# Sending rows with long ties to a late batch, and one looped copy of the repeat round, in a top-p attention kernel

## The reference, cut to what matters

```python
def _top_p_attention(X, W1, W2, W3):
    logits = (X @ W1.T @ W2.T) @ (X @ W3.T).T
    probs = softmax(logits, axis=-1)
    idx = argsort(-probs, axis=-1)
    sp = take_along_axis(probs, idx, axis=-1)
    cs = cumsum(sp, axis=-1)
    keep_sorted = cs - sp < 0.9          # the fewest largest that reach 0.9
    A = probs * mask(keep_sorted)
    return A / A.sum(-1)
for n in range(2):
    A = _top_p_attention(Xa, W1, W2, W3)
    Xf = R @ Xf                          # R: adj + I, rows normalized
    Xa = A @ Xa
    Z = Z + Xf @ U1[n].T + Xa @ U2[n].T
```

## Time and profile before

| | us |
|---|---|
| median of 3 runs | 2774.62 (2766.83 to 2774.76) |
| the profiled execution | 2770.99 |
| its span | 2769.2 |
| PE busy | 2355.1 (85%) |
| DVE busy | 2199.7 (79%) |
| ACT busy | 1072.5 (39%) |
| POOL busy | 141.5 (5%) |
| mean granted TensorE clock | 0.934 of full |

### The profile page before, as it was taken

One profiled execution on the slowest core, in us unless ns is written; L12 is line 12 of the kernel. 1 busy time (PEld: TensorE's weight loads), 2 busy tenths in 40 slices (PEclk: granted clock), 3 DMA queues, 4 the chain that ended last, 5 costly groups with the idle time before them and its releaser, 6 DMA issues. The chain is left out here.

```text
span 2769.2 us, 53551 instructions
## 1 busy us (share of the span) xinstructions
PE 2355.1 (85%) x17759; PEld 1987.9 (72%) x17759; DVE 2199.7 (79%) x6636; ACT 1072.5 (39%) x1785; POOL 141.5 (5%) x353
## 2 busy tenths in 40 slices
PE   5899998777888887888886649996999999999985
PEld 1566666555767776777775549995999999999952
DVE  2777777279888888888889777766999999999836
ACT  4566666433333333333333130003343443434423
POOL 0000000101111110000000010000000000000000
PEclk9999999997999998999997869998999999999997
DMA  3000000020222221222220235543334343433220
GB/s 128 2 2 1 1 1 2 1 89 17 95 100 100 100 100 51 100 100 101 100 100 14 87 128 202 202 164 127 126 108 143 101 146 104 141 110 134 94 88 25
DMA packets 57106, 245.00 MB, mean 88 GB/s; under 512 B 6705, under 2 KB 18352, under 8 KB 43120
## 3 DMA queue, kind: packets, MB, share of 16 engines
q1 hardware_dynamic: 56816, 241.94, 24.9%
HBM read 235.10 MB, written 6.82 MB: 87 GB/s over the span
## 5 line engine op out<-in xcount | busy, mean ns | idle before, releaser
L1932 PE MATMUL a_acc<-H,pT 128*128 128x128 f32 x4056 | 547.8, 277 | 11.7 <-ACT a_rows L1964 3.8
L1932 PEld LDWEIGHTS a_acc<-H,pT 128*128 128x128 f32 x4056 | 495.3, 192 | 28.7 <-DVE pT L2066 19.9
L935 PE MATMUL small<-XR,wT 128*128 128x128 f32 x2756 | 375.9, 282 | 28.3 <-ACT wT L1131 27.5
L71 DVE MAX8 cand<-e 128x8 f32<-128x64 f32 (+3 forms) x1898 | 302.7, 240 | 101.4 <-issue 101.2
L819 PE MATMUL lg<-kT,qs 128*128 128x512 f32 (+1 forms) x742 | 339.9, 596 | 50.5 <-ACT e L1075 38.5
L935 PEld LDWEIGHTS small<-XR,wT 128*128 128x128 f32 x2756 | 341.6, 196 | 44.4 <-ACT wT L1131 44.4
L2066 DVE TENSOR_TENSOR pT<-a_tr,a_adjT 128x512 f32<-128x512 f32 (+1 forms) x546 | 316.3, 643 | 22.5 <-PE a_tr L1891 19.3
L839 PE MATMUL accR<-XR,adj 128*128 128x129 f32 x2704 | 327.2, 283 | 0.0
L839 PEld LDWEIGHTS accR<-XR,adj 128*128 128x128 f32 x2704 | 324.1, 200 | 0.0
L1891 PE MATMUL a_tr<-ident,prob 128*128 128x128 f32 x2028 | 311.2, 274 | 10.9 <-ACTq L1958 10.9
L1131 ACT ACTIVATE wT<-tr 128x512 f32<-128x512 f32 (+1 forms) x371 | 206.2, 566 | 273.1 <-PE tr L925 271.4
(11 more groups left out here) (334 smaller groups left out, 2457.1 us busy)
## 6 DMA issues: line engine op xcount, KB each, us to landing
adj<-in_adjT SPq DMA_DIRECT2D x52, 1664.0 KB, 7.3
g_adj<-in_adjT SPq DMA_DIRECT2D x26, 1664.0 KB, 6.9
a_adj<-in_adj SPq DMA_DIRECT2D x26, 1664.0 KB, 6.8
a_adjT<-in_adjT SPq DMA_DIRECT2D x156, 256.0 KB, 3.9
a_adjT<-in_adjT SPq DMA_DIRECT2D x26, 128.0 KB, 4.2
XT<-in_x_t SPq DMA_DIRECT2D x1, 1664.0 KB, 13.5
hT_scratch<-hT SPq DMA_DIRECT2D x1, 1664.0 KB, 12.2
nsT_scratch<-nsT SPq DMA_DIRECT2D x1, 1664.0 KB, 5.8
```

What stands on the lines that cost most here:

```text
L71: eng.max(cand[:, n, :], src[:, n * seg:min((n + 1) * seg, width)])
L935: mm = eng.matmul(accA[:, :], wT[(k * NC + c - 1) % 2][:, o:o + P], xa[:, j, 0:P], start=(j == 0), stop=(j == T - 1))
L1932: mm = eng.matmul(acc[:, :], pT[g % RING][:, (j % 4) * P:(j % 4 + 1) * P], H[:, j, :], start=(j == 0), stop=(j == T - 1))
```

## The change

1. `end` computes `late`, whether a partition's own `counts[:, 1, 0:1]` is over 80 (`ROOM_FOR_TIES`). Where `late` is 0, the `backward` rows that are known are counted as open too (`gone`), so that they ask for a slot in the batch, and `backward` becomes 0 for `strict` and `cut_dropped`. The levels are taken with `sharp`, the old `strict`. The three sums of `counts` stand after this.
2. `assign_slots` copies `late` of partition 0 beside the flags and loads it into a register; `select` in step 1 runs `drop_ties` only if it is over 0. The batch runs it as before.
3. In `divide`, the `Fori(0, 3)` ahead of `while_over` is gone, and `another_round` has its ten halvings as a hardware loop.

```diff
+ROOM_FOR_TIES = 80
...
         if spills:
             eng.tensor_scalar(self.counts[:, 0, 0:2], all_of("known"), 0.5, None, ALU.is_lt)
+            eng.tensor_scalar(self.one("late", 0), self.counts[:, 1, 0:1], float(ROOM_FOR_TIES), None, ALU.is_gt)
...
+            if spills:
+                late, base, opened = self.one("late", 0), self.counts[:, 1, 0:1], self.counts[:, 0, 0:2]
+                eng.tensor_tensor(all_of("sharp"), all_of("partial"), all_of("backward"), ALU.subtract)
+                eng.scalar_tensor_tensor(all_of("gone"), all_of("backward"), late, all_of("backward"),
+                                         ALU.is_gt, ALU.mult)
+                eng.tensor_scalar(all_of("backward"), all_of("backward"), late, None, ALU.mult)
+                eng.drain()
+                eng.tensor_tensor(opened, opened, all_of("gone"), ALU.max)
...
-        eng.tensor_tensor(all_of("levels"), all_of("levels"), all_of(strict), ALU.mult)
+        eng.tensor_tensor(all_of("levels"), all_of("levels"), all_of("sharp" if spills else strict), ALU.mult)
...
-        step = FIRST_STEP
-        for n in range(ROUND_HALVINGS):
+        with eng.Fori(0, ROUND_HALVINGS):
             eng.scalar_tensor_tensor(spare, cand, self.round_mid[:, :].bitcast(F32), cand, ALU.is_ge, ALU.mult,
-                                     accum_out=self.mass[:, n, k:k + 1])
...
+                                     accum_out=one("r_mass"))
+            eng.tensor_scalar(one("r_half"), one("r_step"), 0.5, None, ALU.mult)
             eng.drain()
+            eng.tensor_tensor(one("r_up"), one("r_mass"), one("r_theta"), ALU.is_ge)
+            eng.scalar_tensor_tensor(one("r_low"), one("r_mass"), one("r_theta"), one("r_mass"), ALU.is_lt, ALU.mult)
+            eng.tensor_tensor(self.round_back[:, :], self.round_mid[:, :], one("r_half"), ALU.subtract)
             eng.drain()
+            eng.scalar_tensor_tensor(self.round_mid[:, :], one("r_up"), one("r_step"), self.round_back[:, :],
                                      ALU.mult, ALU.add)
+            eng.tensor_tensor(one("r_hi"), one("r_hi"), one("r_low"), ALU.max)
             eng.drain()
+            eng.tensor_copy(one("r_step"), one("r_half"))
+            eng.drain()
...
                 eng.drain()
-                with eng.Fori(0, 3):
-                    with eng.If(eng.snap(flag) > OPEN - 1):
-                        another()
                 while_over(eng, flag, OPEN - 1, self.width // 8, another)
...
-            if both_ways:
+            if late is not None:
+                with eng.If(eng.snap(late) > 0):
+                    self.drop_ties(eng, k)
+                    eng.drain()
+            elif both_ways:
                 self.drop_ties(eng, k)
...
+                        eng.tensor_copy(find.flag_int[:, 2:3], find.one("late", 0)[0:1, :])
...
+                        eng.reg_load(late, find.flag_int[0:1, 2:3])
```

More of the change, by code:

```diff
@@ L95 @@
              "r_above0", "r_theta", "r_below", "r_was", "r_stays", "r_moves", "r_tau", "r_hi", "r_value", "r_bound",
-             "r_above", "r_known", "r_up", "r_mass")
+             "r_above", "r_known", "r_up", "r_mass", "r_step", "r_half", "r_low", "gone", "late", "sharp")
     def __init__(self, sb, width):
@@ L115, in __init__ @@
         self.flag_top = sb("pair_flag_top", [1, 2])
-        self.flag_int = sb("pair_flag_int", [1, 2], I32)
+        self.flag_int = sb("pair_flag_int", [1, 3], I32)
         self.counts = sb("counts", [P, 2, 4])
@@ L290, in end @@
         eng.tensor_scalar(all_of("backward"), all_of("partial"), 0.5, None, ALU.is_lt)
[L291 to L296, removed]
         eng.drain()
@@ L312, in end @@
         eng.drain()
+        if spills:
+            eng.tensor_tensor(self.counts[:, 1, 1:2], base, opened[:, 0:1], ALU.add)
+            for n in (2, 3):
+                eng.scalar_tensor_tensor(self.counts[:, 1, n:n + 1], opened[:, 0:1], base, opened[:, 1:2],
+                                         ALU.add, ALU.add)
         if not both_ways:
             eng.tensor_copy(all_of("strict"), all_of("partial"))
-        eng.tensor_tensor(all_of("levels"), all_of("levels"), all_of(strict), ALU.mult)
+        eng.tensor_tensor(all_of("levels"), all_of("levels"), all_of("sharp" if spills else strict), ALU.mult)
         eng.tensor_scalar(all_of("scale"), all_of(strict), 2.0 ** -24, 1.0 - 2.0 ** -24, ALU.mult, ALU.add)
@@ L353, in another_round @@
         eng.tensor_tensor(one("r_stays"), one("r_stays"), one("known"), ALU.max)
-        step = FIRST_STEP
-        for n in range(ROUND_HALVINGS):
+        eng.memset(one("r_hi"), 0.0)
+        eng.memset(one("r_step"), float(FIRST_STEP))
+        eng.drain()
+        with eng.Fori(0, ROUND_HALVINGS):
             eng.scalar_tensor_tensor(spare, cand, self.round_mid[:, :].bitcast(F32), cand, ALU.is_ge, ALU.mult,
-                                     accum_out=self.mass[:, n, k:k + 1])
-            back = -(step // 2) if n + 1 < ROUND_HALVINGS else 0
-            eng.tensor_scalar(self.round_back[:, :], self.round_mid[:, :], float(back), None, ALU.add)
+                                     accum_out=one("r_mass"))
+            eng.tensor_scalar(one("r_half"), one("r_step"), 0.5, None, ALU.mult)
             eng.drain()
-            eng.tensor_tensor(one("r_up"), self.mass[:, n, k:k + 1], one("r_theta"), ALU.is_ge)
+            eng.tensor_tensor(one("r_up"), one("r_mass"), one("r_theta"), ALU.is_ge)
+            eng.scalar_tensor_tensor(one("r_low"), one("r_mass"), one("r_theta"), one("r_mass"), ALU.is_lt, ALU.mult)
+            eng.tensor_tensor(self.round_back[:, :], self.round_mid[:, :], one("r_half"), ALU.subtract)
             eng.drain()
-            eng.scalar_tensor_tensor(self.round_mid[:, :], one("r_up"), float(step), self.round_back[:, :],
+            eng.scalar_tensor_tensor(self.round_mid[:, :], one("r_up"), one("r_step"), self.round_back[:, :],
                                      ALU.mult, ALU.add)
+            eng.tensor_tensor(one("r_hi"), one("r_hi"), one("r_low"), ALU.max)
             eng.drain()
-            step //= 2
-        eng.tensor_scalar(self.low[:, 0:ROUND_HALVINGS, k], self.mass[:, 0:ROUND_HALVINGS, k], one("r_theta"), None, ALU.is_lt)
+            eng.tensor_copy(one("r_step"), one("r_half"))
+            eng.drain()
+        eng.tensor_scalar(self.round_mid[:, :], self.round_mid[:, :], float(FIRST_STEP >> ROUND_HALVINGS), None, ALU.add)
         eng.drain()
-        eng.tensor_tensor(self.low[:, 0:ROUND_HALVINGS, k], self.low[:, 0:ROUND_HALVINGS, k], self.mass[:, 0:ROUND_HALVINGS, k], ALU.mult)
-        eng.drain()
-        eng.tensor_reduce(one("r_hi"), self.low[:, 0:ROUND_HALVINGS, k], AX.X, ALU.max)
         eng.scalar_tensor_tensor(spare, cand, self.round_mid[:, :].bitcast(F32), cand, ALU.is_lt, ALU.mult)
@@ L451, in keep, with select @@
                                  accum_out=self.one("kept", k))
-    def select(self, eng, k, e_pad, kind, flag, regs, both_ways, found=False):
+    def select(self, eng, k, e_pad, kind, flag, regs, both_ways, found=False, late=None):
         def another():
@@ L1272, in _ @@
                 regs = [eng.alloc_register(f"group_flag{q}") for q in range(4)]
+                late = eng.alloc_register("late_flag")
                 eng.memset(kT[DA:P, :], 0.0)
@@ L1319, in assign_slots @@
                         eng.drain()
-                        eng.scalar_tensor_tensor(find.flag_int[:, :], find.both("over_full")[0:1, :], float(OPEN),
+                        eng.tensor_copy(find.flag_int[:, 2:3], find.one("late", 0)[0:1, :])
+                        eng.scalar_tensor_tensor(find.flag_int[:, 0:2], find.both("over_full")[0:1, :], float(OPEN),
                                                  find.flag_top[:, :], ALU.mult, ALU.add)
@@ L1339, in read_flags @@
                         eng.wait_ge(flagT_ready, turn_of(step, p) + 1)
-                        eng.tensor_reduce(find.flag_int[:, :], flagT[:, :, :], AX.X, ALU.max)
+                        eng.tensor_reduce(find.flag_int[:, 0:2], flagT[:, :, :], AX.X, ALU.max)
                         eng.drain()
@@ L1346, in select @@
                         find.select(eng, k, e[b][k][:, :], kinds[k], flag, regs, step == 1,
-                                    found=step == 1 and not at(p, PAIRS))
+                                    found=step == 1 and not at(p, PAIRS),
+                                    late=late if step == 1 and not at(p, PAIRS) else None)
                         if step == 1:
```

## The result

The changed kernel takes 3186.37 us (median of 4 runs, 3184.47 to 3186.88) against 2771.32 for the kernel before (4 runs): 1.150 times as long, 95% interval 1.148 to 1.152. The forecast was 3290 in a range from 3070 to 3620. The profiled execution took 3186.65 us, its span is 3184.9, against 2770.99 and 2769.2 before: 415.7 us more.

What follows compares the result with a forecast made beforehand. It took DVE and PE as nearly level, DVE leading by little. From 2771, gains of 33, over-full pairs of 347 and empty turns of 204 gave 3289, forecast as 3290 us, range 3070 to 3620.

Steps and rivals of the forecast that it cites:

- `late` is always 0; 159 rows ask for 128 slots; pairs 9, 11 and 12 overflow: Step 1: one partition's base can't exceed 26, so no pair drops; six tiles run eight repeat rounds.
- A repeat round, 40.6 us: One round on DVE in an over-full tile, built from its parts: 40.6 us, bounds 30 and 60.
- Gains, pairs 0 to 8: -32: Drops left out save DVE net 6 us a pair; PE uses only its waits, 28 to 29, plus 3 for its clock.
- The over-full pairs without their empty turns: 162, 90 and 95: us added in pairs 9, 11 and 12 by selects and repeat rounds while PE waits; sum 347.
- 2s: Empty turns of a pair's two tiles; s, 21 turns in one tile, was put at 2 to 6 or 40 to 100 us.
- The empty turns, +204: Nest turns after a tile's last round: three of six tiles stall at 3 us a turn, 3 x 63 and 3 x 5.
- The cheap end: Lower bound for an empty turn of the nest that doesn't stall: 0.1 or 0.3 us, 5 us for 21 turns.
- the first rival: Empty turns of the nest are cheap in all six tiles, 6 x 5 us: 3115 us in all; chance 0.22.
- some 3.8 slow tiles of six: A body of 160 instructions straddles a block edge in some 0.6 of places; the sum would be some 45 us more.
- The case's sign: Slower 0.92, same 0.01, faster 0.07; not slower if the batch never overflows, 2730, or the limit holds, 2747.

Runs made afterwards that it cites:

- no_drop: The kernel before without the drop pass in the 26 tiles of step 1, long-tied rows staying out of the batch; 2729.36 us, ratio 0.9843.
- unrolled: The changed kernel with the ten halvings of a repeat round unrolled in place of the hardware loop, the operations the same; 3176.44 us.
- limit80: The changed kernel with the limit of 80 compared with the batch's rows summed over all partitions, not one partition's base; 2749.01 us, ratio 0.9905.
- by_place: The changed kernel with the drop fixed in the code to pairs 7 to 10 and no limit computed or loaded; 2725.89 us, ratio 0.984.
- limit90: The changed kernel with a limit of 90 compared with the batch's rows summed over all partitions; 2738.70 us, ratio 0.9881.
- short_code: The kernel before with the third part of the change alone: no Fori(0, 3), the ten halvings as a loop; 2757.13 us, ratio 0.9946.
- exps_first: by_place with ACT's two exponentials of pair p + 2 ahead of its propagation-row copies in pairs 0 to 5; 2737.36 us, ratio 0.9872.
- three_first: The changed kernel with the Fori(0, 3) put back ahead of the nest, so a second copy of the round's body; 3129.93 us.

## Why the prediction was right, and where it was off

- **`late` is always 0; 159 rows ask for 128 slots; pairs 9, 11 and 12 overflow.** Right, shown by the trace of after (one drop, six tiles with rounds, three and one in pair 9 and one in each of the others, eight in all) and by the limits of 80 and 90. The sum of 159 itself is counted, not measured; the runs bound it where they could, at the limits.
- **A repeat round, 40.6 us.** Measured 41.5. The loop's share was 0.36 us a halving where I had taken 0.25. The 128-wide MAX8, which the trace of before didn't have, took 0.197 us a segment (5.13 for 26), between its two neighbours as taken.
- **Gains, pairs 0 to 8: -32.** Measured -30.3. Inside it the terms miss, and the misses cancel; that the sum comes out is luck. Pairs 0 and 1 gave 6.7 for 8.6. Pair 6 gave 8.9 where I had about 13: I let `select` be the only thing between the rows and `attend` and overlooked ACT's exponentials, due at the same moment. Pairs 7 and 8 gave 9.5 for 5, in `no_drop` as well, which has the old code of the rounds, so the shorter jump isn't the reason. It is PE's granted clock behind a wait that is gone; for the same matmuls PE is busy 58.7 us for 61.6 in pair 7 and 61.2 for 63.8 in pair 8. Here are the 13 us behind the flags of pair 7, after and before, PE's clock being the eighth column (stretch, us, busy us of PE, PEld, DVE, ACT, POOL, clock, DMA share, GB/s):

```profile
1082.20:1095.20 13.00, 11.03 (x92) 10.20 (x91) 11.38 (x88) 1.92 (x6) 2.26 (x5) 1.00 0.14 35
```

```profile
1103.00:1116.00 13.00, 11.58 (x72) 10.60 (x70) 12.76 (x101) 1.54 (x4) 5.18 (x13) 0.74 0.01 2
```

  The first row block, 52 matmuls, took 5.97 us after and 7.89 before (timeline of PE, after and before):

```profile
1086.40 5.97 PE L851 MATMUL accR<-XR,adj 128*128 128x129 f32 x52
```

```profile
1108.16 7.89 PE L839 MATMUL accR<-XR,adj 128*128 128x129 f32 x52
```

  I had allowed 3 us for the clock in all.
- **The over-full pairs without their empty turns: 162, 90 and 95.** With the gaps as measured (15.3 us in tile 18, 16.5 to 17.4 in the other five), 2s is 32.6, 33.9 and 33.7, and the sums come to 195, 124 and 129; measured 193.4, 123.9 and 126.9. Part of each gap (2.5 us) I had counted in the round already.
- **The empty turns, +204.** This is the term that failed, mis-sized by 119.5 us, and with it the mechanism that I held likeliest: 21 turns took 14.3 us in each of five tiles and 19 took 13 in the sixth, 84.5 us for 124 turns of 0.68. I took half of the tiles to stall at 3 us a turn, from gaps at long jumps, and none did. The rows that I used as an upper bound were jumps over some 440 instructions (by my count of the code) and over the body of the pair loop; none was a jump to and fro over a short body, again and again. The cheap end was too cheap as well: I had 0.1 to 0.3 us, and the turn with its two jumps, counter and test of the flag is 0.68; the 5 us that I had for 21 turns that don't stall are 14.3. Without that term's error the sum is about 3170, 16 under the measured 3186. So what came true is the condition of the first rival, cheap turns everywhere, which I gave 0.22: its 3115 is 71 us too low, my 3290 104 too high. The measured time lies between the two, inside the range.
- **The rule of the Trainium skill** ("Runtime: NRT & Kernel Launch", "Instruction fetch mechanics"), by which a branch out of the two-block window stalls, gave me some 3.8 slow tiles of six. That count was an estimate with a step of my own: it takes a block just left to be out of the window, which the page doesn't say, and a body that straddles one edge lies in two blocks. No tile stalled, in the shorter body of some 85 recorded operations or in the unrolled one of some 160, so the runs speak against that step and not against the rule. That a jump over code costs more when the code is longer does agree: the gaps before `drop`, behind the rounds, are 28.2 us with the long code and 10.7 with the short; those before `keep`, at the same jump once the drop is gone, are 21.9 us in the changed kernel, 39.6 unrolled and 60.1 with two copies (all from 600 us on). So the length counts for the jump forward, which is taken once, and the runs show no such price for a repeated jump back into code just left.
- **The case's sign.** Not slower was to come only if the limit held or the batch had room. With the limit holding it came: 2749 where I had put 2747; with all drops gone 2729 where I had 2730. Both are closer than their working. I had 28 us gained by pair 6 and 4 lost later, and in `limit80` 20.8 were gained by the flags of pair 7 (1082.14 for 1102.90) and 4.2 more in pairs 7 and 8; and the 2729 are of the old, long code.

## What to carry to other kernels

Before a limit is put on a counter, ask over what the counter runs: this one held one partition's rows, and only the matmul with ones summed it, so a limit of 80 guarded a value that can't pass 26. A fallback for overflow that is never run has no row in the trace; price it from its parts, for here three over-full pairs cost 444 us, ten times what the change could gain, and count from the inputs how often it will be met. Spend a scarce resource (slots of the batch) in the places where the engine that it relieves is the bound: `by_place` with nine drops beats `limit90` with eleven by 13 us, 12 of them in the two pairs that DVE sets.

## What the runs showed of the hardware that was not expected

- After a wait of only 2.44 us PE's granted clock was 0.74 over the next 13 us (1.00 is 2.4 GHz, 0.50 is 1.2), and 1.00 where the wait was gone; the row block behind it took 7.89 us in place of 5.97. The same pair 7 shows it in every kernel. With a wait at its flags it took 67.9 us (`before`, 2.44), 66.4 (`short_code`, 2.35), 69.0 (`exps_first`, 2.09) and 69.7 (`three_first`, 0.84); in the eight without one it took 65.0 to 65.2 at a clock of 1.00. So the pair took 1.3 to 4.7 us more behind a wait, and the loss didn't follow the wait's length.
- A turn of a loop that does nothing but test a register, jump over a body of some 85 recorded operations (drains not counted) and come back costs 0.68 us, with little change for the unrolled body of some 160 (100.2 and 104.5 us for the same 124 turns).
- A short DVE loop of nine small operations leaves a gap of 0.34 to 0.36 us before each turn after the first; unrolled, a round of ten turns is 2.2 us shorter. Against that stand 17.7 us of longer gaps ahead of `keep` in the unrolled kernel: over eight rounds the two prices were equal on DVE.
- The gaps behind a jump over a block that isn't run grow with the block in number and in size. Ahead of the drop they were 1.7 us at 17 of 27 tiles over the long block and 1.8 at 6 over the short one. Ahead of `keep` they were 1.2 at 19 in the changed kernel, 2.1 at 19 unrolled, 3.0 at 20 with two copies, and 2.4 at 23 in `no_drop`, up to 6.3 us for one.
